# One load instead of four for the inverted softmax sums of a group of four heads

## What is computed

```
o1 = _attn(q, k1, v1, causal[None, None])
...
o2 = _attn(q, ks, vs)
...
o3 = _attn(q, kw, vw, winmask[None, None])
g = gate[:, :, None, None, None]
o = g[:, 0] * o1 + g[:, 1] * o2 + g[:, 2] * o3
```

## Time and profile before

| | us |
|---|---|
| median of 3 runs | 984.56 |
| lowest and highest of them | 983.65, 985.37 |
| span of the profiled execution | 980.1 |

### The profile page before, as it was taken

How to read it: one execution, slowest core, us unless ns; L and a number is a source line. 1 busy time by engine, 2 the same in 40 slices (tenths; PEclk the granted TensorE clock), 3 DMA queues, 4 the chain that set the end, 5 groups by cost and what they waited for, 6 DMA issues and landing times.

```text
span 980.1 us, 22296 instructions
## 1 busy us (share of the span) xinstructions
PE 875.3 (89%) x9216; PEld 588.9 (60%) x9216; DVE 595.7 (61%) x1666; ACT 457.1 (47%) x764; POOL 204.5 (21%) x274
## 2 busy tenths in 40 slices
PE   9888798999999999999999999999988879978876
PEld 8675475566666665666566566656555555644553
DVE  5545534673688468845884588558844764653456
ACT  1003326453555355525543655356435645524754
POOL 1002100120225012401341124112411231131122
PEclk9999689999999999999999999999979999998988
DMA  7100000000000000000000001000100100030000
GB/s 198 25 7 1 1 6 23 23 23 28 23 23 23 28 23 23 23 28 23 23 23 28 7 23 39 23 1 23 39 11 26 36 23 23 23 81 23 2 1 22
DMA packets 25572, 25.84 MB, mean 26 GB/s; under 512 B 14688, under 2 KB 20576, under 8 KB 25344
## 3 DMA queue, kind: packets, MB, share of 16 engines
q1 hardware_dynamic: 25472, 24.42, 8.7%
HBM read 19.69 MB, written 4.72 MB: 25 GB/s over the span
## 4 chain that ended last, share of the span: by engine, by line
PE 58%; DVE 17%; ACT 11%; issue 6%; DMA 5%; POOL 2%; SPq 1%; POOLq 0%; DVEq 0%; ACTq 0%
PE ring L934 7%; PE pv L955 5%; PE side_a L633 5%; PE ring L889 5%; PE pv L973 4%; ACT pr L1190 4%; DVE rden L1676 3%; DMA scale<-branch_scale 3%; PE heads L879 2%; PE side_a L642 2%; PE heads L914 2%; PE ring L929 2%; DMA branch_scale<-rden 2%; PE heads L861 2%; PE ring L897 2%
## 5 line engine op out<-in xcount | busy, mean ns | idle before, releaser
L1190 ACT ACTIVATE pr<-ring 128x1024 f32<-128x1024 f32 (+1 forms) x128 | 120.9, 944 | 108.3 <-PE ring L938 61.0
L934 PE MATMUL ring<-kq 64*128 64x256 f32 (+2 forms) x1280 | 136.5, 341 | 0.7 <-ACT kq L1242 0.5
L934 PEld LDWEIGHTS ring<-kq 64*128 64x128 f32 x1280 | 96.3, 191 | 42.6 <-issue 30.8
L1234 ACT ACTIVATE kq<-ring 128x896 f32<-128x896 f32 x64 | 58.8, 919 | 85.3 <-PE ring L889 85.3
L1686 DVE SCALAR_TENSOR_TENSOR ob<-pv,all_gates,scale 128x256 f32<-128x256 f32 x96 | 46.3, 482 | 85.3 <-PE pv L973 38.4
L1661 DVE TENSOR_REDUCE toks<-heads 128x2 f32<-128x512 f32 x64 | 44.3, 692 | 84.8 <-PE heads L919 83.4
L573 POOL TENSOR_TENSOR toks<-ta,tb 128x128 f32<-128x128 f32 (+1 forms) x96 | 39.7, 434 | 180.4 <-DVE tb L1652 180.4
L1242 ACT ACTIVATE kq<-ring 128x256 f32<-128x256 f32 x64 | 24.6, 384 | 107.5 <-PE ring L897 107.0
L1676 DVE RECIPROCAL rden<-pv 128x256 f32<-128x256 f32 x32 | 56.2, 1756 | 25.5 <-PE pv L955 25.0
L536 POOL TENSOR_TENSOR oT<-ob 128x256 f32<-128x256 f32 x32 | 23.3, 727 | 226.3 <-DVE ob L1686 226.3
L889 PE MATMUL ring<-early,toks 128*128 128x128 f32 x448 | 63.5, 284 | 7.5 <-ACT pr L1190 7.4
(11 more groups left out here) (377 smaller groups left out, 1704.4 us busy)
## 6 DMA issues: line engine op xcount, KB each, us to landing
scale<-branch_scale SPq DMA_DIRECT2D x128, 96.0 KB, 2.3
branch_scale<-rden SPq DMA_DIRECT2D x32, 128.0 KB, 1.7
late<-in_late SPq DMA_DIRECT2D x1, 2158.5 KB, 8.4
xin<-in_x SPq DMA_DIRECT2D x16, 64.0 KB, 2.2
pr<-in_prep SPq DMA_DIRECT2D x1, 602.0 KB, 3.8
y<-ob SPq DMA_DIRECT2D x8, 64.0 KB, 1.9
kq<-in_masks SPq DMA_DIRECT2D x1, 480.0 KB, 8.5
toks<-in_final SPq DMA_DIRECT2D x1, 434.0 KB, 4.4
```

Of the source, the lines that this page charges most:

```text
L934: m = pe.matmul(ring[:, j, at:at + nq], kq[rows, k, key0:key0 + P], kq[rows, k, Q + q_:Q + q_ + nq], start=r % 2 == 0, stop=at > P)
L1190: act.activation(out, in_, ACT.Exp, scale=SCALE).then_inc(S("exp_done"), 1)
L1234: act.activation(kq[:, k, :], flat[:, 0:WIDE], ACT.Copy).then_inc(S("turned"), 1)
```

## The change

The four loads of a group, one for each head, become one load. On the side of `scale` it covers all 128 partitions with 768 contiguous elements each. On the side of DRAM it names four rows (one per head, 32 rows of `branch_scale` apart), each read 32 times, each reading 768 contiguous elements. Bytes and destinations are the same, 384 KB for a group. The count that DVE waits for falls from 64 to 16 a group.

```
-                    for j in range(4):
-                        sp.dma_start(scale[32 * j:32 * j + 32, :, :], scale_out[32 * j:32 * j + BR, :].unsqueeze(0)
-                                     .broadcast_to((32, BR, T))).then_inc(S("scale_loaded"), 16)
+                    sp.dma_start(scale[:, :, :].rearrange("p b t -> p (b t)"),
+                                 scale_out.rearrange("(j r) t -> j (r t)", j=4)[:, 0:BR * T].unsqueeze(1)
+                                 .broadcast_to((4, 32, BR * T))).then_inc(S("scale_loaded"), 16)
...
-                    dve.wait_ge(S("scale_loaded"), of * 256 + 64 * g + 64)
+                    dve.wait_ge(S("scale_loaded"), of * 64 + 16 * g + 16)
```

## The result

The changed kernel takes 1097.75 us (median of 4 runs, 1094.61 to 1105.36), beside 984.96 us for the kernel before: a ratio of 1.1135, 95% interval 1.1057 to 1.1212. A median here is of all runs of a kernel, while a ratio leaves out slow runs, those more than 1.5% above the fastest of the same kernel, so the two can differ a little. The change makes the kernel slower, as forecast, but by 113 us instead of 30, and outside the forecast range. The profiled execution has a span of 1092.7 us, 112.6 us more than before.

The account below looks back on a forecast made before the run. TensorE, nearly full, was taken as held by hand-overs, with branch 0 starting on the load's landing in 27 of 32 groups. +18.2 us on the chain and +12 us off it gave 984.56 + 30 = 1014.6 us, range 998 to 1036.

Parts of the forecast that it names:

- The bound: TensorE 89% busy, held by hand-overs; branch 0 on VectorE starts when the scale load lands in 27 of 32 groups.
- the five hidden groups: Last groups of images 0 to 4, interval 14.68 us ended by TensorE; 7 us to spare, so they add nothing.
- The issues: On SP, three issues go; the new one may cost 0.55 us instead of 0.42; nothing behind it waited for soon.
- The number of engines: New scale load runs on 4 DMA engines with 98,304 bytes each; sign: DMA share at or under 0.25.
- The landing: New scale load lands 5.7 us after its issue (1.76 + 3.92), against 3.6; interval from inversion to branch 0 9.3 us.
- The groups off the chain: 14 groups starting on the landing but off the chain pass on 0.4 of 30.0 us, +12 us.
- What lies around the span: Time outside the profiled span, 984.56 - 980.1 = 4.5 us, is not touched by the change.
- The granted clock: A TensorE clock below that of the trace would add time that the sum doesn't hold; no size given.
- All engines work: Rival: load shared over 16 engines, landing 2.7 to 3.4 us after the issue, 978 us; chance 0.08.
- Absorbed: Rival: load on 4 engines, but TensorE's other work takes up the delay; 986 us, no measurable change; chance 0.05.
- Crowded rate: Rival: four engines at the lower rate, landing 8.1 us, interval 11.7 us, 1059 us; chance 0.07.
- The change does nothing: Rival: the four issues are hidden anyway; excluded because they stand on the chain; no chance given.

Follow-up runs that it names:

- delay2_off: Kernel before, two scratch-tensor store round trips put before the loads in only the 14 groups that start on the landing but were off the chain: 1041.69 us.
- filled: Kernel after, with 468 matmuls of a constant, results unread, put into 20 of TensorE's gaps: 1069.90 us, ratio 1.0818 to the kernel before.
- rows16: Kernel after, each head's sums written four times so the one load's source has 16 rows outermost, each read 8 times: 978.88 us, ratio 0.991 to before.
- delay1: Kernel before, one store round trip to a scratch tensor put ahead of the four loads in every group: 1046.14 us, ratio 1.0540.
- rows8: Kernel after, each head's sums written twice so the one load's source has 8 rows outermost, each read 16 times: 1010.68 us, ratio 1.0269 to before.
- delay2: Kernel before, two store round trips to a scratch tensor put ahead of the four loads in every group: 1110.54 us, ratio 1.1267.

## Why the prediction was wrong, step by step

**The bound: right.** The same 27 groups start on the landing and none of them hides it; the five hidden groups keep their interval (14.68 and 14.69 us; the last packet of their loads ends 4.6 us or more ahead of the branch).

**The issues: right in size, one thing missed.** The new issue takes 0.53 us, where 0.55 was allowed for. But SP does have something behind it: in one group the loads of `final` (lines 456 to 462) follow at once and share the queue with the longer transfer. That group has the interval of 14.31 us (952.02 to 966.33); the old loads of that group were through in time (7.09 us).

**The number of engines: right.** The share is 0.23, under the 0.25 that was named as the sign. The wait of line 1686 for the load was to reach 80 us or more, and is 138.7 (60.3 + 78.4).

**The landing: the term was too small.** The forecast was 5.7 us from the issue and an interval of 9.3; the mean interval is 10.57, so the landing comes after 6.95 us. Two pieces of it are seen. The first packet comes 0.4 us later than an old load's, and the "1.76 us that don't depend on the size" were taken from old loads. And an engine moved 19.8 and 23.1 GB/s in the two stretches above, not the 25.1 of the tail of a small load: a load's packets of 3072 bytes take 126 to 165 ns on average (249 in the load that meets those of `final`), though the median of most loads is 121 to 128 ns. Why some packets take longer stays open. By the packets, the 27 loads take on average 1.35 us to the first packet, 5.0 us from there to the end of the last, and 0.74 us more to the branch; the 5.0 stands against the 3.92 of the prediction, and this is most of the miss. At the measured intervals the working gives 285.4 - 27 x 9.3 = 34 us more if every group passes all of it on, and 25 us with the share of 0.4 off the chain.

**The groups off the chain: wrong.** They were to pass on 0.4 of their delay, on the ground of waits behind the branch. In delay2_off 48.5 us of delay make the span 60.6 us longer, the clock's part included, and TensorE's idle time alone 33.0 us longer. In filled, where the clock's part is small, all 27 groups together cost 79.7 us of span for 81.0 us of delay, so a share near one fits best; no run has the share of these groups without the clock. What was overlooked is the order on VectorE: `xn`, `m` and `toks`, which feed TensorE, stand right behind branch 0. TensorE's slack at those places was below the delay, and the wait behind the branch that was to absorb it is at another instruction. With the share at 1 the forecast rises by 0.6 x 30.0 = 18 us.

**What lies around the span: 1.9 us, not 4.5.** The runs of the kernel after list time and span together (1094.61 and 1092.7). The 4.5 us came from comparing the profiled execution with the median of other runs. This hardly moves the forecast.

**The granted clock: not in the sum.** The last sentence of the prediction names it, and no term holds it. So the prediction put it at nothing; filled shows some 28 to 33 us of it.

The three add up: 30.2 us forecast, 18.0 for the groups off the chain, 34.4 for the landing, and what is left of the 112.6 us is 30.0. This is a remainder, taken at a share of one; it lies within the bounds that filled gives for the clock. The split of waiting and clock is read off one kernel pair, so it is good to a few us at best; filled itself is still at 0.956 where before is at 0.962.

**The rivals.** *All engines work* was false for the kernel as changed; rows16 makes it true and measures 978.88 us, where 978 had been worked out. That agreement is luck: the landing came later than this rival had it (3.9 us against 2.7 to 3.4), the intervals are not shorter than before, and a gain of 6 us is less than the runs lie apart. A load over all 128 partitions did not bring all engines by itself: the kernel after has a share of 0.23. *Absorbed* is refuted by the waits above. *Crowded rate*: 8.1 us of landing was reached only in the load that meets those of `final`, and its 1059 us lies below the result for the same two reasons as the forecast. *The change does nothing* is refuted by delay1: some 1.6 us a group on this path cost 61 us.

**The range.** It reached to a full share off the chain with a small error of the landing (1036 us). What took the time out of it are the size of the landing (5.7 us forecast, 6.95 measured) and the clock (nothing in the sum, about 30 us measured); the clock was named as a possibility, but no part of the range was given to it.

**What stays open.** Whether rows16 is faster than before at all: the median of its runs is 0.6% lower (978.88 against 984.82 us), and the runs of the two overlap (972.67 to 988.49 and 978.83 to 992.77). Its intervals are 3.6 us longer in sum, while both busy and idle time of TensorE are a little less. Also open is why a us of interval costs 1.0 us in rows8 (30.6 for 30.6) but 1.5 in delay2 (133.6 for 89.4). Longer gaps with more time at the lower clock fit, with a clock of 0.948 and 0.896, but no run here separates the two.

## What to carry to other kernels

When several loads are merged into one, look at the outermost count of both sides in the built program: here a broadcast with four rows outermost ran on four engines, and rows repeated by the producer, as in rows16, brought all sixteen back. When a wait on an in-order engine grows, price everything behind it on that engine that a full engine consumes, not only what its consumers on the chain show. And where the bounding engine is TensorE, give a term to the clock: in the kernel after nearly every gap of over 2 us was paid once as idle time and once more as slow work.

## What the runs showed that was not expected

Constant matmuls in 20 gaps took 28 us off a kernel of 1098 us, though the gaps' causes stayed. A gap of 2.9 us was followed by 3.5 us at a clock of 0.51. The ordinary form of a DMA issue cost a chain of store and loads 1.1 us a group (8.52 against 7.51 us on average) and this kernel 2.2%. And a load of 384 KB to 128 partitions landed in 3.9 us on 16 engines, and in 6.4 us or more on 4.
